# A decoder on one core: distance attention in one written-out order, its grid by a hyperbolic tangent a layer earlier, and a talking-heads output on two 64-row halves

## The reference, cut to what matters

```python
# block l0x, distance attention; q from x, k and v from the context
scores = einsum('bhid,bhjd->bhij', qh, kh) / sqrt(8)
p   = softmax(where(mask, scores, -1e32)) * mask
cum = cumsum(p, -1); tot = sum(p, -1); pos = abs(j - i)
dist   = sqrt(clip((tot - cum) * pos, 0))
gamma  = -softplus(gammas)                     # one number a head
diff   = exp(sigmoid(pdiff))                   # 8 x 128 x 128
effect = clip(exp(dist * gamma * diff), 1e-5, 1e5)
scores = softmax(where(mask, scores * effect, -1e32))
scores[:, :, 0, :] = 0
x = layernorm(x + einsum('bhij,bhjd->bhid', scores, vh) @ Wo.T + bo)

# block l1a, talking heads; 4 memory keys and values a head
dots = 10 * einsum('bhid,bhjd->bhij', l2norm(q), l2norm([mem_k, k]))   # 128 x 132
dots = einsum('hg,bgij->bhij', W_pre, dots), causal
dots = where(dots < 64th largest of the row, -max, dots)
attn = einsum('hg,bgij->bhij', W_post, softmax(dots))
out  = einsum('bhij,bhjd->bhid', attn, [mem_v, v]) * head_scale
x = layernorm(x + (out * sigmoid(x @ Wg + bg)) @ Wo)
```

## Time and profile before

| what | value |
|---|---|
| median of 3 runs | 1494.11 us (1493.06 to 1494.6) |
| the profiled execution | 1494.57 us; its span 1492.4 us, 2.2 us less |
| mean granted TensorE clock | 0.786 of full speed |
| busy of the span | DVE 1049.9 us (70%), PE 927.2 (62%), ACT 605.1 (41%), POOL 126.8 (8%) |
| l0a | 15 to 95 us |
| l0x | 95.3 to 345.7 us |
| l1p, l1w, l1o | 375 to 491, 491.5 to 694.8, 694.8 to 785 us |

### The profile page before, as it was taken

How to read it: one execution, slowest core, us unless ns; L and a number is a source line. 1 busy time by engine, 2 the same in 40 slices (tenths; PEclk the granted TensorE clock), 3 DMA queues, 4 the chain that set the end, 5 groups by cost and what they waited for, 6 DMA issues and landing times. The chain is left out here.

```text
span 1492.4 us, 18333 instructions
## 1 busy us (share of the span) xinstructions
PE 927.2 (62%) x6190; PEld 610.4 (41%) x6190; DVE 1049.9 (70%) x2464; ACT 605.1 (41%) x1211; POOL 126.8 (8%) x259
## 2 busy tenths in 40 slices
PE   4844244345787204245997835899868616867877
PEld 2522122222455103235874522666545304644643
DVE  4867898984565698984336856799659586966842
ACT  2644555550443404244114614665127321644632
POOL 0110000101000000000011130000011021020100
PEclk9975667666898656677998957899869756988967
DMA  5000000001123600001000000000000000000000
GB/s 184 2 1 0 0 0 0 0 0 42 51 67 88 262 0 1 1 0 50 1 1 1 1 0 0 1 0 1 0 1 2 1 0 0 2 1 1 1 1 14
DMA packets 25382, 29.17 MB, mean 20 GB/s; under 512 B 657, under 2 KB 22033, under 8 KB 24274
## 3 DMA queue, kind: packets, MB, share of 16 engines
...
## 5 line engine op out<-in xcount | busy, mean ns | idle before, releaser
L1910 DVE TENSOR_TENSOR_SCAN l2a_hs<-l2a_decay,l2a_b_ps 128x512 f32<-128x512 f32 x64 | 78.0, 1221 | 14.3 <-ACT l2a_decay L1840 6.1
L1765 PEld LDWEIGHTS l2a_b_ps<-l2a_diag,l2a_uT 128*128 128x128 f32 x512 | 64.1, 191 | 39.3 <-issue 38.0
L2323 PE MATMUL l1w_mem_ps<-l1a_rows,l1w_post 128*128 128x64 f32 x16 | 4.3, 363 | 110.6 <-DVE l1a_rows L2464 110.6
L1765 PE MATMUL l2a_b_ps<-l2a_diag,l2a_uT 128*128 128x128 f32 x512 | 69.9, 280 | 1.9 <-DVE l2a_hs L1910 1.7
L1773 PE MATMUL l2a_acc_ps<-l2a_hc,pack 128*128 128x512 f32 x128 | 65.5, 595 | 1.0 <-DVE l2a_hc L1921 1.0
L2437 DVE MATCH_REPLACE8 l1w_minus<-l1w_low,l1w_minus 128x129 f32<-128x129 f32 (+39 forms) x264 | 64.5, 263 | 0.0
L2431 DVE MAX8 l1w_low<-l1w_minus 128x8 f32<-128x129 f32 (+37 forms) x332 | 59.7, 261 | 0.4
L833 PE MATMUL l0x_scores<-pack,l0x_prob 128*128 128x128 f32 x128 | 25.4, 363 | 54.6 <-ACT l0x_prob L968 54.6
L2351 ACT ACTIVATE l1w_score<-l1w_mix_ps 128x264 f32<-128x264 f32 (+7 forms) x29 | 11.4, 447 | 107.2 <-DVE l1a_rows L2464 92.1
L1840 ACT ACTIVATE l2a_decay<-l2a_dt,pack 128x1016 f32<-128x1016 f32 x32 | 36.4, 1141 | 45.5 <-DVE l2a_hs L1910 45.5
L2330 PE MATMUL l1w_at_ps<-l1w_post,l1a_rows 128*128 128x128 f32 x256 | 42.9, 343 | 13.4 <-ACT l1a_rows L2374 13.4
...
## 6 DMA issues: line engine op xcount, KB each, us to landing
scores_dram<-l1p_dots SPq DMA_DIRECT2D x8, 1056.0 KB, 6.4
l1a_rows<-scores_dram SPq DMA_DIRECT2D x8, 1056.0 KB, 13.0
...
```

Source lines behind the costliest of these rows:

```text
L1765: mm = nc.tensor.matmul(bx_ps(n)[:, j * S:(j + 1) * S], uT[:, c, b, :], diag[:, s % 2, b, :], start=True, stop=True)
L1910: nc.vector.tensor_tensor_scan(hs[:, n % 2, :], decay[:, k % 2, batches, :].rearrange("p b t -> p (b t)"), bx_ps(n), 0.0, ALU.mult, ALU.ad ...
```

## The change

It has four parts.

1. **The grid in l0a.** A new class `Distances` is hooked into `attention` for `l0a` alone. In l0a's queues DVE gets three operations of 128 x 16, ACT exp and Ln of 128 x 16 with the table load for Ln and one back, then in each batch's step, behind `copy_out` and ahead of `copy_sums`, one Tanh (scale 0.5) and one Exp (bias 1) of 128 x 128; POOL gets one product of 128 x 128 with `apart` a batch. exp(1 + tanh(p/2)) is exp(2 sigmoid(p)).
2. **l0x.** The prologue is gone. The loop is unrolled, with one order written out for each engine. Transposed probabilities have a bank of their own (`turn_ps`), q, km and v two buffers each. The maximum of a half is one reduction. The two products, with the grid and with the coefficient, become one operation a head of 128 x 128 (16 a batch), with the per-head `rate` = softplus squared over the sum; the sum's square root on ACT is gone. The subtraction of the second maximum is gone from DVE; it is the bias of the last exponential, which becomes 8 operations of 128 x 128 a half.
3. **l1w.** `rows` becomes a ring of three blocks (`ROW_BUFS`). SP's load of block n, from n = 3, waits for `mix_again(n-3)`. Weights are made in place in the ring. `copy_again` writes a new tile `mixed` of 128 x (batch, head) x row, with the last two dimensions exchanged on the way: it reads PSUM at a stride of 128 numbers and writes runs of 4.
4. **l1o.** The values' product streams `mixed[:, b * H + h, :]`, 128 numbers in a row. The memory part is laid on two halves of 64 rows: rows 0 to 63 hold chunks 0 to 3, rows 64 to 127 chunks 4 to 7, issued in turn, in different banks. `mem_v` comes in two transfers of 128 KB, `mem_w` twice, 256 KB each. The number of matmuls is the same.

```diff
+    def act_step(self, act, now):
+        if 0 <= now < B:
+            self.nc.scalar.activation(grid[:, now, :], self.cm.pdiff[:, now, :], ACT.Tanh,
+                                      scale=0.5).then_inc(self.tanh_set, 1)
+        if 0 <= now - 1 < B:
+            act.wait_ge(self.tanh_set, now)
+            self.nc.scalar.activation(grid[:, now - 1, :], grid[:, now - 1, :], ACT.Exp,
+                                      bias=1.0).then_inc(self.twice_exp, 1)
...
+                    nc.vector.tensor_tensor(every(rate), every(rate), gamma2[:], ALU.mult).then_inc(rate_set, 1)
+                    for half in range(2):
+                        after(dve, prob_set, 2 * (b - 1) + half + 1)
+                        for h in range(HALF):
+                            last = nc.vector.scalar_tensor_tensor(
+                                out=dist[:, half, h, :], in0=left[:, half, h, 1:W], scalar=rate[:, half, h:h + 1],
+                                in1=grid[:, b, :], op0=ALU.mult, op1=ALU.mult)
...
+                def exponential(b, half):
+                    for h in range(HALF):
+                        last = nc.scalar.activation(prob[:, half, h, :], dist[:, half, h, :], ACT.Exp,
+                                                    bias=last_mx[:, half, h:h + 1], scale=scale)
...
+                    if n >= ROW_BUFS:
+                        sp.wait_ge(at_mm, (ROWS_K // 4) * (n - ROW_BUFS + 1))
+                    sp.dma_start(blocks[n % ROW_BUFS][:], scores_dram.rearrange("b g i j -> (b g) i j")[:, r, :]) \
...
-                        nc.scalar.activation(rows[:, i:i + 4, 0:128], at_ps[u % 2][:], ACT.Copy).then_inc(at_set, 1)
+                        nc.scalar.activation(mixed[:, :, i:i + 4], at_ps[u % 2][:].rearrange("p i h -> p h i"),
+                                             ACT.Copy).then_inc(at_set, 1)
...
+                for part in range(2):
+                    p = slice(64 * part, 64 * part + 64)
+                    sp.dma_start(mem_v[p, :], cm.A["l1a_mv"][:, part * 512:part * 512 + 512]).then_inc(w_in, 16)
+                    sp.dma_start(mem_w[p, :, :], mem_dram.rearrange("(b h) m i -> (h m) b i", b=B)).then_inc(mem_in, 16)
...
-                            nc.tensor.matmul(out, chunk(mem_v, c), mem_w[:, b, :], start=c % 4 == 0, stop=False,
-                                             skip_group_check=True)
+                        for c in range(TCH // 2):
+                            for part in range(2):
+                                p = slice(64 * part, 64 * part + 64)
+                                nc.tensor.matmul(chunk(o_ps[b % 2], c + part * (TCH // 2)), chunk(mem_v, c)[p, :],
+                                                 mem_w[p, b, :], start=c == 0, stop=False, skip_group_check=True)
...
-                                                  v_all[:, b, h * E1:(h + 1) * E1], rows[:, :, b * H + h],
+                                                  v_all[:, b, h * E1:(h + 1) * E1], mixed[:, b * H + h, :],
```

More of the change, by code:

```diff
@@ L805, in score @@
+                    nc.tensor.matmul(qk_ps[:, 1, :], w("wk"), cm.ctxT[:, b, :], start=True,
+                                     stop=True).then_inc(qk_mm, 1)
                 def score(b, half):
                     pe.wait_ge(qk_set, b + 1)
-                    if not distance:
-                        after(pe, probT_set, 2 * b + half - 1)
+                    after(pe, scaled_set, 2 * (b - 1) + half + 1)
+                    bank = lambda g: scores[:, half, HH * (g % 2):HH * (g % 2) + HH, :]
@@ L809, in score @@
                     pair = (2 * half, 2 * half + 1)
[L810 to L816 removed]
+                    for g in pair:
+                        nc.tensor.matmul(bank(g), cm.ident_bf[:], bcast_mid(cm.masks[mask], HH), start=True, stop=False)
@@ L828, in score, with transpose_probs @@
                     mm.then_inc(scores_mm, 1)
[L830 removed]
+                def transpose_probs(b, half, part):
                     pe.wait_ge(prob_set, 2 * b + half + 1)
[L832 to L836 removed]
@@ L847, in weigh, with project_v @@
+                    for n in range(HH):
+                        mm = nc.tensor.transpose(turn_ps[:, n, :], prob[:, half, HH * part + n, :], cm.ident)
+                    mm.then_inc(turn_mm, 1)
+                def project_v(b):
+                    after(pe, oT_set, b - 1)
+                    nc.tensor.matmul(v_ps, cm.ctxT[:, b, :], w("wv"), start=True, stop=True).then_inc(v_mm, 1)
                 def weigh(b, half):
```

756 lines of the change are left out of this document (289 added, 467 removed).

## The result

The kernel before took 1493.59 us (median of 4 runs, 1492.59 to 1494.6), the changed one 1448.12 (median of 4, 1437.94 to 1449.38). The ratio is 0.9679, with an interval of [0.9646, 0.9713]. Forecast were 1444 us and a range of 1428 to 1466. The profiled execution of the changed kernel took 1447.14 us over a span of 1445.4; the span before was 1492.4.

A forecast was written before the change was run, and what follows sets the result against it. DVE was taken to bound l0x and PE l1o. Terms 0.8 (l0a) - 34.0 (l0x) + 1.5 (l1w) - 18.1 (l1o) = -49.8 us took the profiled 1494.57 to 1444.8, forecast as 1444; range 1428 to 1466.

The forecast's parts named there:

- l0x, prologue: Start of l0x: the copy of q can start at 98.1 instead of 109.46 us, so -11.3 us.
- l0x, the loop: l0x's batches on DVE: 23.9 us each instead of 27.5; first scan to last second score 185.9 instead of 212.3, -26.4.
- the rival that priced them at 0.34: l0x's batch longer: small products at 0.34 us, ACT's chain half a microsecond more; 13.4 us in all, total 1457; chance 0.15.
- wait for ACT: In each l0x batch DVE waits 3.7 us for second root, table load, first effect and hand-overs; small work hides there.
- l0x, the end: Behind l0x's last shift: split exponentials and transposes through one bank add 3.7 us to 14.3, between 0 and twice that.
- l1w: Block l1w: ring loads just hidden and copies with exchanged dimensions near 0.60 us each; +1.5 us for the whole block.
- transposing-copy rival: In l1w the copy with exchanged dimensions costs twice its price: 20 x 0.6 = +12 us, total 1456; chance 0.06.
- the slower case: In l1w a copy of 3.1 us instead of 0.60 cancels the gain; at 3.3 the total is 1498; chance 0.02.
- just hidden; n = 5 and 7 are alike: l1w's ring load for n = 3 lands at 581.2, ACT wants the result at 582.58; n = 5 and 7 likewise.
- l1o: Block l1o: values' product 2.15 us, memory part 1.27; -2.3 a batch, start +0.5, together -18.1 us.
- stays at 3.8: In l1o the values' product does not gain, the column halves sharing something other than the strided read; total 1457; chance 0.15.
- l0a: Block l0a: small added work on DVE, POOL and ACT, mostly in gaps; +0.8 us at the block's end.

The follow-up runs named there:

- grid_in_l0x: Changed kernel with the grid made at the start of l0x for all batches at once, nothing of it in l0a: 1442.51 us, ratio 0.9668.
- products_unfused: Changed kernel with l0x's grid and coefficient products apart again, four operations of 128 x 1024 a batch: 1443.61 us, ratio 0.9668; l0x 220.8.
- root_first: Changed kernel with ACT's first root in l0x ahead of the fourth copy, the sums' copy behind the second root: 1444.23 us, ratio 0.9681; l0x 217.1.
- warm_between: Changed kernel with 42 unread matmuls a batch in l0x, 22 of them between the transposes: 1443.37 us, ratio 0.967; l0x 214.6.
- exp_in_halves: Changed kernel with l0x's last exponential one operation a half again, second maximum subtracted by DVE: 1456.1 us, ratio 0.9746; l0x 228.6.
- strided_values: Changed kernel with `mixed` laid row by head, copies contiguous, values' product reading every 512 bytes: 1469.24 us, ratio 0.985; l1o 93.1.
- no_ring_loads: Changed kernel without SP's ring loads of blocks n = 3 to 7 in l1w, their mixed scores not computed: 1439.8 us, ratio 0.9639; l1w 204.2.
- changed_again: The changed kernel run once more with no edit, as base for the other runs: 1442.25 us, ratio 0.9668 to the kernel before.

## Why the prediction was right, and where its terms were off

The total came out 4 us above the forecast, inside the range; -47.0 of span against -49.8. That it came so near is in part luck, since larger errors cancelled (see the end of this section). Point by point:

- **l0x, prologue: right.** -11.3 forecast; 119.24 to 106.72, less what came before l0x, is -11.6. grid_in_l0x shows the reason: DVE is freed of the grid.
- **l0x, the loop: right in sum.** 185.9 forecast, 186.1 measured. The products at 0.267 were right (0.268), and so the rival that priced them at 0.34 falls. The Trainium skill ("VectorE: DVE Perf Modes", on the TRN2 errata) advises against small tiles, since each instruction pays a fixed cost. The trace agrees: eight products of 128 columns take 2.14 us, one operation of 1024 takes 1.22. But the eight do in one pass what took two, so 16 in 4.29 us were no loss against the large ones (some 4.6 in products_unfused). The step that was mis-sized is the **wait for ACT, 3.7 forecast, 4.55 measured**: I counted the root as starting with its data, while the last copy of transposes and the table load stand ahead of it in ACT's queue. Either mend shortens it, the other order (root_first: 3.97) or faster transposes (warm_between: 3.5). The scans (4.54, forecast 4.7) and the second scores (4.93, forecast 5.2) were a little shorter, and the first two batches took 23.1 each, so the sum held.
- **l0x, the end: the largest miss.** +3.7 forecast with 7.4 as its upper bound, +7.0 measured. The mechanism, split exponentials and one bank for all transposes, was named without a price for either: the exponentials made 2.4 of it, and the transposes and copies that alternate in one bank 5.1, less 0.5 in the rest. At the granted 0.50 four transposes take 1.1 us; the end before, on which the forecast rests, ran at 0.74 (331.5 to 345.7 us). warm_between gives back 1.1 of the 7.0, and there PE came 1.8 us late to the output projection (293.75 to 295.58), behind unread matmuls, so the clock's part may be larger.
- **Which part did it.** The prediction's sum implied that moving the subtraction to ACT's bias counts, and exp_in_halves shows that (+8.8 when undone). That fusing the products counts was implied too, and it hardly does (1.0). The rest of the batch's gain, 2.2 of 3.3 us, the rows place in the new order of DVE's queue and the waits for PE that went with it; no run undoes that, so it is argued and not shown.
- **l1w: mis-sized, +1.5 forecast, +5.6 and +3.5 measured.** The price of the copy was right (0.60; 0.598), so the transposing-copy rival and with it the slower case fall. The Trainium skill ("SBUF — State Buffer", on cachelines) says of matmuls that PSUM accesses which aren't contiguous slow them; ACT's copy, of which it doesn't say so, shows no such cost, 0.598 against 0.597 in strided_values. The wrong step is "just hidden; n = 5 and 7 are alike". They are alike: from the end of the transposes to ACT's want there were 6.5 us at n = 3, and in the same trace 6.3 and 6.1 at n = 5 and 7. The load does land in 5.1 of them. But I set the landing against ACT's want and left out PE's mixing, which comes between: the block of n = 5 lands at 603.56, and ACT's first copy starts at 605.41. 1.3 to 1.9 us of mixing don't fit into the 1.0 to 1.4 that were left. Against no_ring_loads each of the three blocks lost by its load: n = 3 0.5 (1.5 in changed_again), n = 5 2.7, n = 7 2.0. Some 1.6 of the +5.6 have another cause, ahead of the first maxima, which stays open.
- **l1o: right, slightly better.** Stride was the cause, as argued from the 32-wide tiles: 1.89 forecast as 2.15, 1.96 at 8 bytes, 4.7 with a stride of 512 bytes. The rival "stays at 3.8" falls. The memory part took 1.10, not 1.27: 0.069 a pass, where l1p's 132-column ones took 0.079; what makes that difference is not shown. The start cost +1.6 and not +0.5: all of PE, the gates too, waits for the second half of `mem_v`, which is issued behind the first copy of `mem_w`.
- **l0a: not to be told.** +0.8 forecast, between -1.4 and +0.5 over the runs, less than unchanged blocks vary.

Errors of opposite sign helped: l0x was 3.3 worse than forecast, l1w 4.1, against 1.4 better in l1o, 1.7 before l0x and 1.8 behind l1o. The last two are spread of blocks that the change touches little or not at all.
